# Where the row pieces of a decoder layer stand between its score blocks: one wait moved, activations put at blocks' ends

## The chip, the cores and the metric

The kernel runs on one core of a Trainium2 chip, as one launch. Its engines are TensorE (PE, with its weight loads PEld), VectorE (DVE), ScalarE (ACT), GpSimd (POOL) and SyncE (SP, which here only issues transfers). The metric is the device time of one execution in microseconds; less is better.

## The reference

A post-norm decoder layer in fp32, x of 2 x 1024 x 512, a context of 2 x 2048 x 512: linear attention, cross attention with softmax over 16 heads of 32, and a mixture of 8 experts, each token going to two of them, with a capacity of 640 rows for each expert. Each part is added to its input and normalised.

```python
q = jax.nn.elu(q) + 1.0;  k = jax.nn.elu(k) + 1.0          # linear attention
kv = jnp.einsum('bthd,bthe->bhde', k, v)
out = num / jnp.clip(denom, 1e-06, None)[..., None]
...
dots = jnp.einsum('bhnd,bhmd->bhnm', q, k) * SCALE          # cross attention
attn = jax.nn.softmax(dots, axis=-1)
...
logits = xf @ router_w + router_b                           # experts
topk_p, topk_i = jax.lax.top_k(probs, K)
keep = rank < cap
h = jax.nn.gelu(jnp.einsum('ecd,edf->ecf', buf, w1) + b1[:, None, :], approximate=False)
eo = jnp.einsum('ecf,efd->ecd', h, w2) + b2[:, None, :]
...
x = _layernorm(x + _L0_attn_ref(...)); x = _layernorm(x + _L0_xattn_ref(...)); x = _layernorm(x + _L0_ffn_ref(...))
```

## The kernel before

One Python loop writes a plan, a list of stages with keys, and each engine then walks the whole plan and does its own share of every stage. So the order of the plan is the order in each engine's queue, and semaphores between the engines say when a share may start. The stages of the span, roughly: linear attention and the projections of the context until 540 us, the cross attention loop until 1535, the expert phase until the end.

The loop has 16 turns, each a group of 4 heads by 512 queries, over 2048 keys. A turn has 8 blocks, and each block handles two key tiles (`s`, `s + 1`). The order in a block is the string `BLOCK` (line 50): eight "score" units for the next block, each a matmul of 128 keys by 512 queries that ScalarE turns into exponentials (`score`, line 1834), and eight "max" units, each a matmul whose row maximum VectorE takes (`take_max`, line 1488), for a turn further on. Scores rotate through three PSUM banks, maxima and all side pieces through three others. Behind the units come the numerator matmuls of the current tiles (line 1225), the denominators of an earlier pair (line 1243), now and then ScalarE's copy of a finished numerator or denominator (lines 1841 and 1847), GpSimd's addition of a pair of tiles (line 1956), and VectorE's reciprocals (line 1508). For the last tiles VectorE does the pair additions. The last maxima are over in turn 14, so that the blocks behind it hold scores alone.

The shift of a turn (the row maxima, brought into the query stack) is made of `shift_high`, `shift_low` and `shift`; `shift` is a small TensorE matmul (line 1203) in the maxima's banks, a few blocks after a turn's last maximum.

Between these, "side pieces" finish the rows of (b, h), 512 rows of batch b. A generator, `rows_of`, yields the kind of its next piece, and the block loop takes at most one piece without TensorE in the middle of a block (in front of its tenth unit) and, if none was taken there, one with TensorE at its end; in the last three turns both. The pieces are: the projections of four tiles (`rows`), the router's sums (`parts`), VectorE's inverse roots (`row_root`, `row_shift`), ScalarE's normalisation of each of four tiles (`x2`, line 1853), the logits, the two best experts (`route_top`, in which VectorE subtracts the best logit and ScalarE takes the exponential, line 1866), the counts, ranks, weights and slots, the one-hot matrices (`hot`) and their product (`table`). Three of the four row groups run beside the loop: (0,0) from turn 8, (0,1) from turn 10, (1,0) from turn 13; (1,1) comes behind it.

At the loop's start `second_stack` loads the second stack of keys and what the rows need (`load_xwo`: two weight matrices of 1 MB, three small tables, bxo_cols the last of them). Then `zero_counts` clears three tiles on VectorE and scales the router's weights by bxo_cols, for which it waits for all of `load_xwo`:

```python
dve.wait_ge(*xwo_in[()])
dve.wait_ge(*const_in[()])
V.tensor_tensor(router_scaled[:, :, :], router_pad[:, :, 1:1 + E],
                bxo_cols[:, :].unsqueeze(2).to_broadcast([P, NC, E]), ALU.mult) \
    .then_inc(counts_zero.sem, 1)
```

router_scaled is read by the stage `fold_turn`, in turn 1 (turns count from 0; the change's title calls it turn two).

Of the kernel before, what the change touches and what calls it, by code (L numbers as in the profile page):

```python
# [27 lines left out]
HT = NT // NH  # L28
# [21 lines left out]
BLOCK = 6 * ("max", "score") + ("score", "max", "score", "max")  # L50
WITH_PE, WITHOUT_PE = "with TensorE", "without TensorE"
EARLY, LATE, WHOLE = "early", "late", "whole"
# [71 lines left out]
def program(nc, t):  # L124
    ctx = ExitStack()
    with ctx:
# [165 lines left out]
        def chunk_of(b, mc):  # L292
# [44 lines left out]
        den_summed, den_copied = signal("den_summed"), signal("den_copied")  # L337
        counts_zero, folded = signals_on("fold_done", 2)
        folds_summed, folds_turned = signals_on("folds_summed", 2)
# [56 lines left out]
            "zero_counts": lambda: (counts_zero,),  # L396
            "fold": lambda: (folds_summed, fold_copied),
            "fold_turn": lambda: (folds_turned, folded),
# [20 lines left out]
            "logits": lambda b, h: (logits_summed, logits_done),  # L419
            "route_top": lambda b, h: (logits_shifted, router_exp),  # L420
            "route_counts": lambda b, h: (chosen_ready, before_ready),
# [263 lines left out]
        def rows_of(b, h):  # L685
            yield WITHOUT_PE
            do("fetch_parts", b, h)
            yield from project_rows(b, h, WHOLE)
            yield WITH_PE
            begin_parts(b, h)  # L690
            do("parts", b, h)
            yield WITHOUT_PE
            do("row_root", b, h)
            yield WITHOUT_PE
            do("row_shift", b, h)
            for k in range(HT):
                do("x2", b, h, k)
                if k < HT - 1:
                    yield WITHOUT_PE
            do("store_x2", b, h)  # L700
            yield WITH_PE
            do("logits", b, h, ring=next_s_bank)
            for stage in ("route_top", "route_counts"):
                yield WITHOUT_PE
                do(stage, b, h)
            yield WITH_PE
            do("ranks", b, h, ring=next_s_bank)
            yield WITHOUT_PE
            do("route_weights", b, h)
            yield WITHOUT_PE  # L710
            do("route_slots", b, h)
            for k in range(TOPK):
                yield WITHOUT_PE
                do("hot", b, h, k)
            yield WITH_PE
            do("table", b, h, ring=next_s_bank)
# [22 lines left out]
        clock = 0  # L739
# [98 lines left out]
        shifts = []  # L838

        def due_shifts(until):  # L840
            while shifts and shifts[0][0] <= until:
                shift(shifts.pop(0)[1], next_s_bank)
# [8 lines left out]
        for turn, (n, h) in enumerate(turns):  # L851
            b, g = groups[n]
            stay = stay_of[turn]
            for s in range(0, MT, 2):
# [10 lines left out]
                for u, unit in enumerate(BLOCK):  # L865
                    if u == len(BLOCK) // 2 + 1:
                        busy = side(WITHOUT_PE)
                    if unit == "max":
                        maxima(1)
                    else:  # L870
                        scores((BLOCK[:u].count("score"),))
# [20 lines left out]
                denominators(clock)  # L892
                postponed(clock)
                if not end:
                    do("add_pair", turn, s + 1)
                    pending.append((clock + 1, turn, s + 1))
# [30 lines left out]
        do("logits", b, h, ring=next_s_bank)  # L927
        do("route_top", b, h)
        do("route_counts", b, h)
        do("route_weights", b, h)  # L930
# [118 lines left out]
        def _(_eng):  # L1049
# [100 lines left out]
            def fold_turn():  # L1150
                out = free_bank("fold_turn")
                pe.wait_ge(*fold_copied[()])
                pe.wait_ge(*counts_zero[()])
                for g in range(NG):
# [187 lines left out]
        def _(_eng):  # L1342
# [167 lines left out]
            def zero_counts():  # L1510
                V.memset(before[:, :, :], 0.0)
                V.memset(head_w[:, :, :], 0.0)
                V.memset(table[:, :, :], 0.0)
                dve.wait_ge(*xwo_in[()])
                dve.wait_ge(*const_in[()])
                V.tensor_tensor(router_scaled[:, :, :], router_pad[:, :, 1:1 + E],
                                bxo_cols[:, :].unsqueeze(2).to_broadcast([P, NC, E]), ALU.mult) \
                    .then_inc(counts_zero.sem, 1)

# [187 lines left out]
            def final_dve_rows(q):  # L1707
                dve.wait_ge(*final_root[q // (PIECES_Y // 2)])
                for n in range(q * TILES_Y, (q + 1) * TILES_Y):
# [9 lines left out]
                    "add_pair": add_pair, "invert": invert, "zero_counts": zero_counts, "rows": rows,  # L1719
                    "row_root": row_root, "row_shift": row_shift, "fold_turn": fold_turn, "logits": logits,  # L1720
                    "route_top": route_top, "route_counts": route_counts, "route_weights": route_weights,
# [8 lines left out]
        def _(_eng):  # L1730
# [132 lines left out]

            def route_top(b, h):
                act.wait_ge(*logits_shifted[b, h])
# [35 lines left out]
            def final_act_rows(q):  # L1901
                act.wait_ge(*final_root[q // (PIECES_Y // 2)])
                for n in range(q * TILES_Y, (q + 1) * TILES_Y):
# [9 lines left out]
                    "shift_high": shift_high, "shift": shift, "score": score, "copy_num": copy_num, "copy_den": copy_den, "x2": x2,  # L1913
                    "x1_logits": x1_logits, "fold": fold, "parts": parts, "route_top": route_top, "turn_xe": turn_xe,
                    "split_w1": split_w1,
# [357 lines left out]
```

## Time and profile before

| | |
|---|---|
| median of 3 runs | 2078.73 us (2077.09 to 2081.12) |
| profiled execution | 2077.5 us, its span 2075.7 us |
| TensorE busy | 1934.5 us (93%) |
| VectorE, ScalarE, GpSimd busy | 1224.6, 883.8, 791.5 us |
| chain that ended last | TensorE 79%, VectorE 12%, transfers 3%, ScalarE 2% |
| granted TensorE clock, mean | 0.969 of full |

All rows are from one execution with the profiler, in microseconds from the start of its span. A busy engine is not one at its peak: matmuls overlap, so the start of one to the start of the next says more than their durations. In a row's brackets stands how long its engine (or the queue in front of it) had idled, and who released it.

### The profile page before, as it was taken

How to read it: one execution, taken by the hardware profiler on the slowest of the kernel's cores; microseconds unless marked ns; L12 is line 12 of the kernel's file. 1: busy time of each engine (PE TensorE's matmuls, PEld its weight loads, DVE VectorE, ACT ScalarE, POOL GpSimd, SP SyncE). 2: the span in 40 equal slices, each digit the busy share in tenths (PEclk: the TensorE clock that was granted, in tenths of full speed). 3: DMA queues.
4: the chain of work that ended last, by engine and by line, in shares of the span. 5: the costliest groups of instructions: out<-in, count | busy, mean ns of one | idle time of the engine just before them, and what ended most of it. 6: DMA issues, size and time to landing. Idle time of an engine off the chain costs nothing.

```text
span 2075.7 us, 26455 instructions
## 1 busy us (share of the span) xinstructions
PE 1934.5 (93%) x10152; PEld 1273.9 (61%) x10152; DVE 1224.6 (59%) x2279; ACT 883.8 (43%) x1587; POOL 791.5 (38%) x705
## 2 busy tenths in 40 slices
PE   6999999989499999999999999999988999999992
PEld 5876666677355555555544544544437988889992
DVE  5565553257276787777767867867753444444433
ACT  3212322222165565666546545545734333334431
POOL 3002200000066777777656746756202222322112
PEclk9999999999799999999999999999988999999996
DMA  7002524583602122322324424332224444444415
GB/s 251 30 1 106 178 81 143 184 215 115 185 17 62 37 72 63 80 55 52 94 65 107 97 63 119 91 87 72 82 82 142 132 107 128 132 111 108 117 21 182
DMA packets 119070, 211.04 MB, mean 102 GB/s; under 512 B 10608, under 2 KB 28672, under 8 KB 118864
## 3 DMA queue, kind: packets, MB, share of 16 engines
q1 hardware_dynamic: 108416, 185.39, 30.1%
q0 software_dynamic: 9440, 21.86, 5.4%
q10 hardware_dynamic: 1088, 2.10, 0.3%
q8 instruction: 80, 1.31, 0.3%
q14 instruction: 46, 0.38, 0.1%
HBM read 147.15 MB, written 62.42 MB: 101 GB/s over the span
## 4 chain that ended last, share of the span: by engine, by line
PE 79%; DVE 12%; DMA 3%; ACT 2%; SPq 2%; issue 1%; POOL 0%; ACTq 0%; POOLq 0%; DVEq 0%
PE banks L1059 34%; PE banks L1314 11%; PE banks L1225 11%; PE banks L1195 9%; DVE max L1488 9%; PE banks L1214 7%; PE banks L1243 5%; PE banks L1065 2%; ACT probs_sum L1834 1%; DMA k_parts<-out_lo 1%; DMA wv_raw<-in_wv_t 1%; DMA bxo_cols<-in_bxo_cols 1%; DMA k_half<-in_xwk_t 0%; PE banks L1133 0%; ACT probs_add L1834 0%
## 5 line engine op out<-in xcount | busy, mean ns | idle before, releaser
L1488 DVE TENSOR_REDUCE max<-banks 128x1 f32<-128x512 f32 x1024 | 628.5, 682 | 188.0 <-PE banks L1195 187.4
L1956 POOL TENSOR_TENSOR probs_sum<-probs_sum,probs_add 128x512 f32<-128x512 f32 x464 | 581.9, 1285 | 352.2 <-PE banks L1225 352.2
L1195 PE MATMUL banks<-k_stack,q_stack 98*128 98x512 f32 x1024 | 430.2, 427 | 32.2 <-DVE max L1488 30.6
L1834 ACT ACTIVATE probs_sum<-banks 128x512 f32<-128x512 f32 x512 | 264.9, 604 | 330.4 <-PE banks L1214 329.7
L1214 PE MATMUL banks<-q_stack,k_stack 98*128 98x512 f32 x1024 | 378.4, 400 | 15.1 <-ACT probs_add L1834 14.7
L1195 PEld LDWEIGHTS banks<-k_stack,q_stack 98*128 98x128 f32 x1024 | 192.9, 188 | 222.6 <-DVE max L1488 100.5
L1834 ACT ACTIVATE probs_add<-banks 128x512 f32<-128x512 f32 x512 | 271.9, 612 | 0.5 <-PE banks L1214 0.5
L1214 PEld LDWEIGHTS banks<-q_stack,k_stack 98*128 98x128 f32 x1024 | 192.9, 189 | 75.3 <-ACT probs_add L1834 25.9
L1998 POOL DMA_INDIRECT y_rows<-eo,tok x40 | 79.5, 1987 | 218.1 <-DVE eo L1687 167.6
L1225 PE MATMUL banks<-probs_sum,v_grp 128*32 128x512 f32 x1024 | 142.7, 619 | 0.0
L1225 PE MATMUL banks<-probs_add,v_grp 128*32 128x512 f32 x1024 | 139.1, 605 | 0.0
L1243 PE MATMUL banks<-probs_sum,ones 128*32 128x512 f32 x1024 | 137.2, 598 | 0.8 <-DVE probs_sum L1503 0.8
L1674 DVE TENSOR_TENSOR hid_lo<-hid,hid_hi 128x640 fp32r<-128x640 f32 x64 | 52.8, 826 | 142.4 <-ACT hid_hi L1899 142.4
L1059 PE MATMUL banks<-w_hi,hid_hi 128*128 128x512 f32 x320 | 128.7, 402 | 0.0
L1059 PE MATMUL banks<-w_hi,hid_lo 128*128 128x512 f32 x320 | 126.4, 395 | 0.0
L1059 PE MATMUL banks<-w_lo,hid_hi 128*128 128x512 f32 x320 | 125.9, 393 | 0.0
L1962 POOL TENSOR_TENSOR x_nat<-x_nat,bxo_row 128x512 f32<-128x512 f32 x16 | 21.1, 1350 | 269.6 <-PE banks L1065 269.6
L1314 PE MATMUL banks<-xe_hi,w_hi 128*128 128x320 f32 x512 | 117.7, 311 | 1.5 <-DVE xe_lo L1658 1.5
L1314 PE MATMUL banks<-xe_hi,w_lo 128*128 128x320 f32 x512 | 117.4, 310 | 0.0
L1314 PE MATMUL banks<-xe_lo,w_hi 128*128 128x320 f32 x512 | 117.4, 311 | 0.0
L1894 ACT ACTIVATE hid<-banks,b1c 128x640 f32<-128x640 f32 x64 | 50.8, 794 | 137.1 <-PE banks L1314 137.0
L1989 POOL DMA_INDIRECT xg<-x_rows,tok x40 | 39.2, 979 | 167.0 <-PE banks L1065 134.4
(233 smaller groups left out, 2782.5 us busy)
## 6 DMA issues: line engine op xcount, KB each, us to landing
k_stack<-k_parts SPq DMA_DIRECT2D x144, 256.0 KB, 4.8
w_raw<-in_L_ffn_w SPq DMA_DIRECT2D x16, 2048.0 KB, 8.4
q_stack<-q_parts SPq DMA_DIRECT2D x48, 256.0 KB
v_grp<-v_rows SPq DMA_DIRECT2D x48, 256.0 KB, 3.2
raw<-in_ctx_t SPq DMA_DIRECT2D x8, 1024.0 KB, 6.4
k_parts<-out_hi SPq DMA_DIRECT2D x32, 256.0 KB, 2.5
k_parts<-out_lo SPq DMA_DIRECT2D x32, 256.0 KB, 2.9
v_rows<-pre SPq DMA_DIRECT2D x32, 256.0 KB, 2.3
```

Of the source, the lines that this page charges most:

```text
L1059: done = nc.tensor.matmul(out, lhsT, rhs, start=start and n == 0, stop=stop and n == len(operands) - 1)
L1195: nc.tensor.matmul(out, queries_of(t)[:, j, tile_of(k)], keys_of(t)[0:STK + SHIFT, j, mc * HALF:(mc + 1) * HALF], start=True, stop=True) \
L1214: nc.tensor.matmul(out, keys_of(t)[0:STK + SHIFT, j, tile_of(s)], queries_of(t)[:, j, :], start=True, stop=True).then_inc(scored.sem, 1)
L1225: done = nc.tensor.matmul(bank(NUM)[j * DH:(j + 1) * DH, :], v_grp[:, s, j * DH:(j + 1) * DH], probs_of(t, s)[:, j, :], start=s == 0, stop ...
L1243: done = nc.tensor.matmul(bank(DEN)[j * DH:(j + 1) * DH, :], ones[:, 0:DH], tile[:, j, :], start=s == 1, stop=s == MT - 1 and tile is tile ...
L1314: done = nc.tensor.matmul(pairs[first][:, h, 0:HC], w, x[:, h * HC:(h + 1) * HC], start=n == 0, stop=n == len(terms) - 1)
L1488: V.reduce_max(max4[:, tiles_of(t), :, :][:, k, j, mc:mc + 1], bank(bank_of["max", t, mc, k, j]), AX.X) \
L1674: V.tensor_tensor(hid_lo[:, f, :], hid[f % 2][:, :], hid_hi[:, f, :].bitcast(F32), ALU.subtract) \
L1834: S.activation(probs_of(t, s)[:, j, :], bank(bank_of["score", t, s, j]), ACT.Exp, scale=SCALE) \
L1894: S.activation(hid[f % 2][:, :].rearrange("p (h n) -> p h n", h=2), pairs[first][:, :, 0:HC], ACT.Gelu, bias=b1c[:, e, f:f + 1]).then_inc( ...
L1956: done = G.tensor_tensor(a[:, j, :], a[:, j, :], b[:, j, :], ALU.add)
L1998: G.indirect_dma_start(out=y_rows, in_=eo[turn % EO][:, :], in_offset=None, compute_op=ALU.add, out_offset=bass.IndirectOffsetOnAxis(ap=to ...
```

## The change

Four edits. The scaling of the router's weights leaves `zero_counts` and becomes VectorE's share of the stage `fold`, in turn 1, with a signal of its own, `router_ready`. A third kind of piece, `AT_END`, stands behind a block's numerators and denominators: the normalisations go there, two and two, with the logits between the pairs, and so does the exponential of the logits, as a stage `route_exp` of its own. `row_shift`, `route_top` and `route_counts` stay in mid-block, with VectorE's share alone. And no piece is taken in mid-block where a shift is due at that block's end.

```diff
@@ rows_of
             do("row_shift", b, h)
-            for k in range(HT):
+            yield AT_END
+            for k in range(HT // 2):
                 do("x2", b, h, k)
-                if k < HT - 1:
-                    yield WITHOUT_PE
-            do("store_x2", b, h)
             yield WITH_PE
             do("logits", b, h, ring=next_s_bank)
-            for stage in ("route_top", "route_counts"):
-                yield WITHOUT_PE
-                do(stage, b, h)
+            yield AT_END
+            for k in range(HT // 2, HT):
+                do("x2", b, h, k)
+            do("store_x2", b, h)
+            yield WITHOUT_PE
+            do("route_top", b, h)
+            yield AT_END
+            do("route_exp", b, h)
+            yield WITHOUT_PE
+            do("route_counts", b, h)
             yield WITH_PE
             do("ranks", b, h, ring=next_s_bank)
@@ the block loop
+        def shifts_due(until):
+            return bool(shifts) and shifts[0][0] <= until
...
                     if u == len(BLOCK) // 2 + 1:
-                        busy = side(WITHOUT_PE)
+                        busy = not shifts_due(clock) and side(WITHOUT_PE)
...
                 denominators(clock)
                 postponed(clock)
+                side(AT_END)
                 if not end:
                     do("add_pair", turn, s + 1)
@@ TensorE, fold_turn
                 pe.wait_ge(*fold_copied[()])
-                pe.wait_ge(*counts_zero[()])
+                pe.wait_ge(*router_ready[()])
@@ VectorE
-                V.memset(table[:, :, :], 0.0)
+                V.memset(table[:, :, :], 0.0).then_inc(counts_zero.sem, 1)
+
+            def fold():
                 dve.wait_ge(*xwo_in[()])
                 dve.wait_ge(*const_in[()])
                 V.tensor_tensor(router_scaled[:, :, :], router_pad[:, :, 1:1 + E],
                                 bxo_cols[:, :].unsqueeze(2).to_broadcast([P, NC, E]), ALU.mult) \
-                    .then_inc(counts_zero.sem, 1)
+                    .then_inc(router_ready.sem, 1)
@@ ScalarE
-            def route_top(b, h):
+            def route_exp(b, h):
                 act.wait_ge(*logits_shifted[b, h])
```

VectorE at the loop's start; before, the scaling stands ahead of all reductions of turns 0 and 1:

```order
L1511 MEMSET before 128x40
L1512 MEMSET head_w 128x128
L1513 MEMSET table 128x80
L1516 TENSOR_TENSOR router_scaled<-router_pad,bxo_cols 128x32
L1488 TENSOR_REDUCE max<-banks 128x1 x32
L1495 TENSOR_REDUCE top<-max 128x16
```

The same place after the change:

```order
L1522 MEMSET before 128x40
L1523 MEMSET head_w 128x128
L1524 MEMSET table 128x80
L1499 TENSOR_REDUCE max<-banks 128x1 x32
L1506 TENSOR_REDUCE top<-max 128x16
L1499 TENSOR_REDUCE max<-banks 128x1 x48
L1529 TENSOR_TENSOR router_scaled<-router_pad,bxo_cols 128x32
```

The scaling has moved behind 80 reductions, ten blocks.

ScalarE in turns 8 and 9 beside the rows (0,0), before; each probs row is four exponentials, y_nat rows are normalisations, rt_ex the logits' exponential:

```order
L1834 ACTIVATE probs_sum_53<-banks 128x512 x4
L1853 ACTIVATE y_nat_64<-y_nat_64,neg_shift,rsqrt_y 128x512
L1834 ACTIVATE probs_add_56<-banks 128x512 x4
L1841 ACTIVATE num_c<-banks 128x512
L1834 ACTIVATE probs_sum_54<-banks 128x512 x4
L1853 ACTIVATE y_nat_64<-y_nat_64,neg_shift,rsqrt_y 128x512
L1834 ACTIVATE probs_add_57<-banks 128x512 x4
L1847 ACTIVATE den_c<-banks 128x512
L1834 ACTIVATE probs_sum_55<-banks 128x512 x4
L1853 ACTIVATE y_nat_64<-y_nat_64,neg_shift,rsqrt_y 128x512
```

And after the change:

```order
L1847 ACTIVATE probs_sum_53<-banks 128x512 x4
L1847 ACTIVATE probs_add_56<-banks 128x512 x4
L1854 ACTIVATE num_c<-banks 128x512
L1866 ACTIVATE y_nat_64<-y_nat_64,neg_shift,rsqrt_y 128x512 x2
L1847 ACTIVATE probs_sum_54<-banks 128x512 x4
L1847 ACTIVATE probs_add_57<-banks 128x512 x4
L1860 ACTIVATE den_c<-banks 128x512
L1866 ACTIVATE y_nat_64<-y_nat_64,neg_shift,rsqrt_y 128x512 x2
L1847 ACTIVATE probs_sum_55<-banks 128x512 x4
L1847 ACTIVATE probs_add_58<-banks 128x512 x4
L1879 ACTIVATE rt_ex<-rt_sv 128x32
```

The four normalisations stood in the middle of four blocks' exponentials, and now stand in twos behind two blocks' exponentials and the copy. In (0,1) the two pairs fall behind blocks without a copy, in (1,0) as here. The pieces from the logits to the table come two or three blocks earlier than before. In SyncE's queue the x1 rows for (1,1) come ahead of the first expert's weights, where they stood behind them; the stores of x2 come ahead of a load of values in (0,0), (0,1) and (1,0).

## Rows read from the trace of the kernel before

**Rows 1.** The page: granted TensorE clock in tenths, 40 slices of the span.
```profile
PEclk9999999999799999999999999999988999999996
```
**Rows 2.** Who waited for whom: in total, times, longest.
```profile
DVE router_scaled L1516 <- DMA bxo_cols<-in_bxo_cols: 28.0, 1, 28.0
...
PE banks L1195 <- DVE max L1488: 30.6, 2, 27.8
```
**Rows 3.** Timeline at the loop's start: start, duration, engine, line, what; idle before.
```profile
540.37 0.39 PE L1195 MATMUL banks<-k_stack,q_stack 98*128 98x512 f32 x1
...
542.85 5.88 SPq L2118 DMA_DIRECT2D k_stack<-k_parts  x12
...
557.64 1.19 SPq L2157 DMA_DIRECT2D bxo_cols<-in_bxo_cols  x1
...
569.76 0.80 PE L1195 MATMUL banks<-k_stack,q_stack 98*128 98x512 f32 x1 [27.76 <-DVE max L1488]
...
573.95 1.07 PE L1225 MATMUL banks<-probs_sum,v_grp 128*32 128x512 f32 x8
```
**Rows 4.** Stretches: length, busy of PE, PEld, DVE, ACT, POOL; clock, DMA share, GB/s.
```profile
541.00:569.00 28.00, 1.00 (x5) 0.48 (x3) 0.09 (x1) 1.91 (x4) 0.00 (x0) 0.59 0.92 222
...
679.00:1010.00 331.00, 330.39 (x1940) 170.21 (x1940) 258.55 (x442) 205.85 (x412) 253.70 (x224) 1.00 0.26 61
```
**Rows 5.** The same view: eight plain blocks, parts, three row groups, three single blocks.
```profile
708.91:763.79 54.88, 54.78 (x323) 28.19 (x322) 42.80 (x74) 34.02 (x69) 42.00 (x37) 1.00 0.20 49
965.61:969.71 4.10, 4.10 (x21) 2.77 (x17) 3.57 (x6) 3.93 (x8) 3.55 (x3) 1.00 0.45 96
1475.08:1479.90 4.82, 4.82 (x33) 2.10 (x32) 4.19 (x8) 4.02 (x10) 0.78 (x1) 1.00 0.20 53
1076.13:1179.06 102.93, 96.04 (x551) 48.61 (x550) 82.77 (x183) 60.03 (x118) 68.31 (x60) 0.98 0.43 106
1244.38:1348.63 104.25, 97.30 (x554) 49.30 (x553) 82.83 (x185) 58.66 (x117) 68.46 (x61) 0.97 0.42 105
1413.82:1491.63 77.81, 71.42 (x424) 34.09 (x423) 58.73 (x124) 48.08 (x97) 33.04 (x31) 0.96 0.28 90
1109.97:1117.95 7.98, 7.88 (x50) 4.42 (x49) 6.37 (x12) 4.80 (x10) 5.43 (x5) 1.00 1.03 307
1302.46:1310.07 7.61, 7.51 (x45) 3.93 (x44) 7.47 (x17) 4.84 (x10) 5.44 (x5) 1.00 0.13 34
1339.70:1348.63 8.93, 8.83 (x58) 5.31 (x57) 8.06 (x16) 4.78 (x10) 5.44 (x5) 1.00 0.83 178
```
**Rows 6.** Timeline, TensorE's waits in turns 8 and 9 beside the rows (0,0).
```profile
1085.39 0.77 PE L1214 MATMUL banks<-q_stack,k_stack 98*128 98x512 f32 x1 [2.87 <-ACT probs_add L1834]
...
1125.23 0.50 PE L1214 MATMUL banks<-q_stack,k_stack 98*128 98x512 f32 x1 [0.89 <-ACT probs_add L1834]
...
1134.46 0.30 PE L1203 MATMUL banks<-identity,max_parts 128*32 128x128 f32 x1 [1.69 <-DVE max L1488]
```
**Rows 7.** ScalarE: first exponentials behind num_c, behind den_c, behind neither; the normalisations' group.
```profile
959.56 0.60 ACT L1834 ACTIVATE probs_sum<-banks 128x512 f32<-128x512 f32 x1 [0.90 <-PE banks L1214]
...
966.38 2.06 ACT L1834 ACTIVATE probs_sum<-banks 128x512 f32<-128x512 f32 x4
...
973.18 2.06 ACT L1834 ACTIVATE probs_sum<-banks 128x512 f32<-128x512 f32 x4 [2.75 <-PE banks L1214]
...
L1853 ACT ACTIVATE y_nat<-y_nat,neg_shift,rsqrt_y 128x512 f32<-128x512 f32 x12 | 10.0, 830 | 7.0 <-DVE neg_shift L1555 7.0
```
**Rows 8.** VectorE, one instruction of route_counts: (0,0), and (1,0) without maxima beside.
```profile
1132.69 0.19 DVE L1589 TENSOR_TENSOR rt_ms<-rt_chosen 128x32 f32<-128x32 f32 x1
...
1459.28 1.18 DVE L1589 TENSOR_TENSOR rt_ms<-rt_chosen 128x32 f32<-128x32 f32 x1
```
**Rows 9.** Issue of the first expert's weights, and ScalarE's first split of them.
```profile
1482.26 0.43 SPq L2189 DMA_DIRECT2D w_raw<-in_L_ffn_w  x1
...
1498.70 1.13 ACT L1880 ACTIVATE w_hi<-w_raw 128x1024 fp32r<-128x1024 f32 x1
```

More of the change, by code:

```diff
@@ L50 @@
 BLOCK = 6 * ("max", "score") + ("score", "max", "score", "max")
-WITH_PE, WITHOUT_PE = "with TensorE", "without TensorE"
+WITH_PE, WITHOUT_PE, AT_END = "with TensorE", "without TensorE", "at the end of a block"
 EARLY, LATE, WHOLE = "early", "late", "whole"
@@ L337, in program @@
         den_summed, den_copied = signal("den_summed"), signal("den_copied")
-        counts_zero, folded = signals_on("fold_done", 2)
+        counts_zero, router_ready, folded = signals_on("fold_done", 3)
         folds_summed, folds_turned = signals_on("folds_summed", 2)
@@ L396, in program @@
             "zero_counts": lambda: (counts_zero,),
-            "fold": lambda: (folds_summed, fold_copied),
+            "fold": lambda: (folds_summed, fold_copied, router_ready),
             "fold_turn": lambda: (folds_turned, folded),
@@ L419, in program @@
             "logits": lambda b, h: (logits_summed, logits_done),
-            "route_top": lambda b, h: (logits_shifted, router_exp),
+            "route_top": lambda b, h: (logits_shifted,),
+            "route_exp": lambda b, h: (router_exp,),
             "route_counts": lambda b, h: (chosen_ready, before_ready),
@@ L838, in program @@
         shifts = []
+        def shifts_due(until):
+            return bool(shifts) and shifts[0][0] <= until
         def due_shifts(until):
-            while shifts and shifts[0][0] <= until:
+            while shifts_due(until):
                 shift(shifts.pop(0)[1], next_s_bank)
@@ L928, in program @@
         do("route_top", b, h)
+        do("route_exp", b, h)
         do("route_counts", b, h)
@@ L1719, in _ @@
                     "add_pair": add_pair, "invert": invert, "zero_counts": zero_counts, "rows": rows,
-                    "row_root": row_root, "row_shift": row_shift, "fold_turn": fold_turn, "logits": logits,
+                    "row_root": row_root, "row_shift": row_shift, "fold": fold, "fold_turn": fold_turn, "logits": logits,
                     "route_top": route_top, "route_counts": route_counts, "route_weights": route_weights,
@@ L1913, in _ @@
                     "shift_high": shift_high, "shift": shift, "score": score, "copy_num": copy_num, "copy_den": copy_den, "x2": x2,
-                    "x1_logits": x1_logits, "fold": fold, "parts": parts, "route_top": route_top, "turn_xe": turn_xe,
+                    "x1_logits": x1_logits, "fold": fold, "parts": parts, "route_exp": route_exp, "turn_xe": turn_xe,
                     "split_w1": split_w1,
```

## The prediction

> **What bounds the kernel.** I read the page's slices first. The TensorE clock row shows 9 nearly everywhere and one 7 in the middle [rows 1]: TensorE sets the pace, with one break. The list of waits names the break: VectorE waited 28.0 us, once, for the transfer of bxo_cols, and TensorE waited 27.8 us in one piece for VectorE's maxima [rows 2]. The timeline shows the order: the first score block begins at 540.37; SyncE issues the second key stack from 542.85 and bxo_cols, the last of that burst, at 557.64; TensorE goes on at 569.76, and the block's numerators start at 573.95 [rows 3]. In 541 to 569 the DMA engines were 92% busy with 222 GB/s; over the 331 us from 679 to 1010 TensorE was busy 330.39 us at full clock [rows 4].
>
> Then I cut the loop at the starts of the numerator matmuls (line 1225), one start per block. Eight plain blocks of a turn take 54.88 us, 6.86 each; the scores-and-maxima part of one is 4.10; a block without maxima takes 4.82 [rows 5]. The three stretches in which a group of rows goes from row_shift to table take longer than their blocks alone: that difference is what the rest of the change can touch.
>
> **Part 1, router_scaled moved to turn two.** It removes one wait and moves one small VectorE instruction (0.19 us for one of its size [rows 8], beside TensorE's work). Without the wait the first block is one like any other: begun at 540.37, its numerators would start 4.10 later, at 544.5. They started at 573.95, so 29.5 us go: 27.8 of wait, the rest matmuls at the low clock after it. The clock was granted at 0.59 over 541 to 569 [rows 4], that is mostly 1.2 GHz, after TensorE had stopped; the first matmul after it took 0.80 us in its row against 0.39 for the same form at 540.37 [rows 3].
> The Trainium skill ("TensorE: Matmul & The Clock Gate", Part 1) says that the low clock is the state of an idle array and that activity lifts it. The trace agrees; by that rule the gain is the wait and a restart, by the wait alone it would be 27.8.
>
> What is late next? The loop reads only stack 0, queries 0 and 1 and values that landed long before. The second stack is first read by turn two's maxima: 32 of turn one's 64 maxima are left, 4 blocks, so about 540.4 + 4 x 6.86 = 568. The stack (16 transfers of 256 KB with its queries, some 4 MB) stands ahead of the 2 MB of weights; at 222 GB/s it is in by about 541 + 18 = 559. Hidden, with 9 us to spare. If transfers slowed to half their rate beside the running engines it would be in at 577, and the cost 9 us: that is the other end. router_scaled itself now waits for the weights at the second block of turn one, about 607; they landed by 569. No queue is moved past: SyncE issues the same burst in the same order.
>
> **Part 2, the side pieces.** Before: (rows 0,0) 102.93 us for 13 blocks, 13 x 6.86 = 89.2, excess 13.7. (0,1) 104.25, excess 15.1. (1,0) 77.81 for 5 blocks with maxima and 6 without: 34.3 + 28.9 = 63.2, excess 14.6 [rows 5]. Sum 43.4.
> Of it TensorE's own matmuls stay: the logits block 7.98 - 6.86 = 1.1, the ranks block 7.61 - 6.86 = 0.75, the table block 8.93 - 6.86 = 2.1 [rows 5]; 3.95 for each of three, 11.8. That leaves 31.6 that come from where the pieces stand. Three kinds show in the waits [rows 6]: TensorE 2.87 us for ScalarE, whose normalisation stood mid-block waiting for row_shift with the exponentials queued behind it (and low clock after it); 0.89 for ScalarE with the logit exponential mid-block; 1.69 of a shift matmul for VectorE's maxima behind route_counts. The change takes each of these places away: the two activations go behind the block's exponentials, VectorE's pieces lose their ScalarE half, and none starts beside a due shift.
>
> What comes in. Two normalisations now stand in a row behind a block's exponentials: 2 x 0.83 = 1.66 us [rows 7]. In a plain block ScalarE idles 2.75 us there, so they are free; behind the numerator copy it idles 0.90, so they cost 0.76; behind the denominator copy no idle time is shown before the exponentials (the row at 966.38 has no bracket), so they cost the full 1.66 [rows 7]. I carry this over to TensorE in full, since its third score bank is taken just as it comes free. Groups (0,0) and (1,0) meet both copies, (0,1) none: 2 x 2.42 = 4.8. Bounds: 0, if the banks absorb it, and 8 x 0.83 = 6.6, if nothing does.
> VectorE's row_shift (7 small instructions, as row_root has) stays mid-block alone; I take 0 for it, between 0 and 2.9 for three (the waits above were ScalarE's). In (1,0) route_counts and ranks share a block, and TensorE must wait for the counts: 1.1, and 1.0 for a slow clock behind it; between 0 and 4. The remaining neighbours (two reciprocals beside route_counts, ranks beside a shift) 1.0, between 0 and 3. Sum of new costs 7.9. Gain 31.6 - 7.9 = 23.7.
>
> At route_counts a rule speaks. The row rt_ms took 0.19 us at 1132.69 and 1.18 at 1459.28 [rows 8], the second in a block without maxima. It has two inputs in SBUF. GpSimd's four pair additions fill 42.00 of the 54.88 us of a plain turn [rows 5], 5.25 of each 6.86, from a little behind the numerators' start; the middle of a block with maxima lies just behind them, that of a block without maxima within them. In the new order of (1,0) this piece moves from the second kind to the first.
> The Trainium skill ("SBUF — State Buffer", SBUF: two separate sides) says VectorE instructions with two SBUF inputs and GpSimd's lock each other out for a whole instruction. By that rule a piece in mid-block of a full block, when GpSimd's four additions are over, is cheap; the row pair agrees. By it the wait for the counts in (1,0) could be near nothing, 2 us less than my sum; I keep the sum.
>
> SyncE's queue is changed too: x1 rows for (1,1) now stand ahead of the first expert weights, 1 MB. Both, 3 MB, were issued at 1482.3, and at the 222 GB/s of the first burst they are in by 1496; ScalarE's first split of the weights ran at 1498.70 [rows 9]. The new schedule is 2 us shorter between the two (the table block is gone from there), so 0.7 us of cover is left: I take nothing, at worst the 1 MB, 4.7 us.
>
> **Sum.** 29.5 + 23.7 = 53.2. The profiled execution took 2077.5 (span 2075.7), so 2024.3 for its like; the median of before is 2078.73, 1.2 above it. I forecast 2025.
>
> **Rivals.**
> (a) The side pieces' gain is mostly lost: normalisations in pairs hold the exponentials, the block stretches, VectorE's pieces fall into GpSimd's additions. For it: the copies' row without idle time. Against: only four of six pairs meet a copy. With new costs at their upper ends (6.6 + 2.9 + 4 + 3 = 16.5) the gain is 15.1 and the time 2034; with half of the old excess kept as well, 2040.
> (b) The burst takes VectorE's place as the bound: TensorE waits for the second stack at about 568. For it: 92% busy DMA engines. Against: the stack is first in the queue. Price 9: 2034.
> (c) More than forecast: the pairs are absorbed, and counts away from GpSimd's additions gives up to 4. New costs near 1: 2017.
> (d) Slower. The place is the stretch after 541: the 28 us of rest is gone and TensorE runs through at full load, and the granted clock sinks for the rest. TensorE is busy nearly all the time in the 1535 us behind it. The gain of 53 is used up where the clock of these is down by 53/1535 = 3.5%; at 4.5% the time is 2094. Against: 331 us without a pause were granted 1.00 [rows 4].
> (e) The change does not do what it says: router_scaled waits again in turn one. It would need weights landing after 607 instead of by 569. Then about 2055 with part 2 alone.
>
> **Chances.** Forecast (2019 to 2031) 0.60; (a) 0.14; (b) 0.06; (c) 0.14; (d) 0.03; (e) 0.03. For its range I take the forecast, (b), most of (c) and the near half of (a): 2016 to 2036. 0.2% is 4.2 us, about what this kernel's runs can tell from no change. Faster 0.96, same 0.01, slower 0.03.
>
> **What would show it.** In the profile of the changed kernel: no wait of VectorE for bxo_cols over 1 us, no 7 in the clock row at 540, numerators of the first block at about 544.5, and the first plain turn's blocks still 6.86. The end of the early rows (the block at 1491.63 before) near 1438. From the numerators ahead of row_shift's block to those behind table's block (0,0) has 11 blocks now, 11 x 6.86 + 3.95 + 2.4 = 81.8 us; (0,1) has 10 and no copies, about 73. TensorE's longest wait for ScalarE's exponentials under 2 us, one in the block with the denominator copy of turns 9 and 14. The tail from the last numerators to the end unchanged within 2 us. I am wrong on part 1 if TensorE waits for k_stack or q_stack near 568, and wrong on part 2 if blocks 9 and 14 with the pairs stretch by more than 2 us each.

## The result, and the profile after

The changed kernel takes 2019.82 us (median of 4 runs, 2017.9 to 2024.36) against 2077.91 for the kernel before, run beside it (4 runs, 2074.19 to 2081.12): ratio 0.9724, 95% interval 0.9701 to 0.9747. The forecast was 2025, its range 2016 to 2036. The profiled execution of after took 2017.9 (span 2016.1); before it was 2077.5 (span 2075.7), so 59.6 us went.

The clock row of after answers to [rows 1]: the 7 behind the first quarter is gone. The 7 late in the row comes from behind the loop, as the 88 did before: there TensorE is busy 9 of 22 us and is granted half of its clock in both kernels.
```profile
PEclk9999999999999999999999999999979999999996
```
Stretches behind the loop, columns as in [rows 4], before (first line) and after:
```profile
1548.00:1570.00 22.00, 9.03 (x36) 7.36 (x36) 13.25 (x54) 5.59 (x9) 6.66 (x7) 0.50 0.46 158
```
```profile
1490.00:1512.00 22.00, 8.60 (x35) 7.15 (x36) 13.13 (x56) 5.87 (x10) 6.38 (x7) 0.50 0.47 156
```
The waits of TensorE from 540 to 1480, the whole loop, answer to [rows 2]: neither the 27.8 us nor any wait for bxo_cols is left.
```profile
PE banks L1070 <- DVE max L1499: 1.7, 1, 1.7
PE banks L1225 <- ACT probs_sum L1847: 1.6, 2, 0.8
PE banks L1254 <- DVE probs_sum L1514: 0.8, 1, 0.8
```
The timeline at the loop's start, against [rows 3] (lines stand 11 to 13 further down in after). The first block begins at 538.81 instead of 540.37 and its numerators follow 4.24 us later, not 33.58. The multiply now stands at 605.11 and waits for nothing.
```profile
538.81 0.39 PE L1206 MATMUL banks<-k_stack,q_stack 98*128 98x512 f32 x1
...
543.05 0.64 PE L1236 MATMUL banks<-probs_sum,v_grp 128*32 128x512 f32 x4
...
605.11 0.18 DVE L1529 TENSOR_TENSOR router_scaled<-router_pad,bxo_cols 128x32 f32<-128x32 f32 x1
```
Stretches of after, columns as in [rows 4]. The first is the stretch of the burst: TensorE busy 28.00 of 28.00 at full clock, beside transfers at 218 GB/s. Then the stretches from row_shift's block to the table block of rows (0,0), 11 blocks, and (0,1), 10 blocks; then four single blocks: row_shift (0,0); second pair of normalisations behind the denominator copy; counts and ranks of (1,0); the one behind it.
```profile
541.00:569.00 28.00, 28.00 (x159) 14.41 (x158) 21.08 (x37) 18.09 (x37) 20.22 (x17) 1.00 0.91 218
1043.56:1124.44 80.88, 79.80 (x472) 41.58 (x471) 71.06 (x162) 50.99 (x101) 57.42 (x50) 1.00 0.49 122
1189.62:1262.38 72.76, 72.46 (x431) 38.36 (x430) 66.07 (x155) 46.91 (x92) 52.45 (x46) 1.00 0.45 116
...
1043.56:1050.38 6.82, 6.82 (x41) 3.45 (x40) 6.54 (x16) 4.06 (x9) 5.45 (x5) 1.00 0.79 172
...
1058.35:1066.35 8.00, 7.22 (x42) 3.30 (x41) 5.46 (x25) 5.15 (x10) 5.00 (x4) 1.00 0.69 201
...
1385.03:1394.16 9.13, 7.43 (x45) 3.96 (x44) 8.21 (x19) 4.92 (x11) 5.44 (x5) 1.00 0.53 170
1394.16:1402.67 8.51, 8.51 (x42) 3.80 (x41) 5.14 (x13) 3.33 (x7) 5.42 (x5) 0.80 0.00 0
```
Predicted for the two long stretches were 81.8 and about 73; they are 80.88 and 72.76. Row_shift's block, 10.39 before, is a plain one. The block that stood at 1491.63 and was foretold near 1438 is at 1433.91.

I name a block by the turn and the first key tile of the numerators that end it: row_shift (0,0) is (8,14), the denominator copy with a pair (9,2) and (14,2), counts with ranks (14,4). Cut at these starts, the profiled executions of all kernels repeat themselves where the work is the same: from (1,6) to (8,12) all fourteen took 422.01 to 422.13 us. Outside the loop they don't. In the eleven that don't wait for bxo_cols, the first numerators start between 540.11 and 545.65; from block (15,2) to the end of the span all fourteen take 582.2 to 585.4. Between them, blocks (1,4) and (1,6) and those beside the rows vary from execution to execution by 1 to 3 us. So a difference of a few us in whole times is no reading of the change, and the experiments below are read by their blocks. Their ratios are to the kernel before, run beside them: its median was 2074.88 for experiments 1, 2 and 7, 2074.07 for 4, 5 and the first of 6, and 2076.12 for 3, the second of 6, and 8.

Where the 59.6 us of the two profiled executions came from:
```
                                         before     after     gone
start of the loop's first numerators     573.95    543.05    30.90
blocks (1,4) and (1,6), the fold          18.17     16.56     1.61
other blocks up to (8,12)                484.01    483.95     0.06
(8,12) to (15,2), the row groups         415.50    390.35    25.15
(15,2) to the end of the span            584.07    582.19     1.88
```

### The profile page after: what moved, and what is told of

The parts are those of the page before. It is cut to its first block, busy times and chain, and to the rows that moved or that the text cites. A ratio compares the mean times of both kernels' runs of the same rounds, so it can differ in the third digit from the quotient of the medians.

```text
span 2016.1 us, 26457 instructions
## 1 busy us (share of the span) xinstructions
PE 1919.1 (95%) x10152; PEld 1268.9 (63%) x10152; DVE 1221.2 (61%) x2279; ACT 882.5 (44%) x1587; POOL 793.8 (39%) x705
## 4 chain that ended last, share of the span: by engine, by line
PE 85%; DVE 10%; DMA 2%; ACT 1%; issue 1%; SPq 0%; POOL 0%; ACTq 0%; POOLq 0%; DVEq 0%
PE banks L1070 36%; PE banks L1236 11%; PE banks L1325 11%; PE banks L1206 10%; PE banks L1225 9%; DVE max L1499 7%; PE banks L1254 5%; PE banks L1076 2%; DMA k_parts<-out_lo 1%; DMA wv_raw<-in_wv_t 1%; DVE stats_y L1707 0%; PE banks L1144 0%; DVE src_lo L1369 0%; DVE wq_lo L1375 0%; ACT src_hi L1754 0%
## 5 line engine op out<-in xcount | busy, mean ns | idle before, releaser
L1697 DVE TENSOR_TENSOR eo<-banks,b2s 128x512 f32<-128x512 f32 x40 | 27.7, 692 | 126.6 <-PE banks L1070 126.6
```

## Experiments

**1. The parts alone.** Part 1 on the kernel before:
```
  V.memset(table[:, :, :], 0.0).then_inc(counts_zero.sem, 1)
+ def fold():
+     dve.wait_ge(*xwo_in[()])   # and the multiply, on router_ready
```


> The kernel before with the first part of the change alone (router_scaled computed at the first fold piece of turn one, with a signal of its own). Theory: the wait of 27.8 us and the restart at the low clock go (30.9 us at the first block's numerators in the changed kernel), and with them the low clock in the fold blocks of turn one (10.09 and 8.08 us before, 9.74 and 6.82 in the changed kernel), so 32.6 us in all: about 2045. Rival: the 1.7 us of the fold blocks come from the second part or from chance; then these blocks measure 10.1 and 8.1 again and the time is about 2047. Second rival: the parts work together (less is gained alone); then over 2050.

Measured: 2046.46 (4 runs), ratio 0.9859 (0.9839 to 0.9880); numerators from 543.23; (1,4) and (1,6) 9.74 and 8.46, where the theory had 9.74 and 6.82 and the rival 10.1 and 8.1, so neither held for both; from (8,12) to (15,2) 417.24, as before but for one slow block. The first part is worth its wait and no more: 30.7 us at the start, of which 29.3 lie in the first block (538.99 to 543.23).

And the changed kernel with part 1 undone, the same edit backwards:

> The changed kernel with the first part undone: router_scaled stands in the loop's first block again, the second part stays. Theory: VectorE waits 28 us for bxo_cols and TensorE 27.8 us for a maximum as before, the fold blocks of turn one measure 10.1 and 8.1 us, and the side blocks keep all of their 25.1 us: about 2052, or 2050 if the 1.9 us behind the loop come too. Rival: the side blocks gain less when the schedule is 32 us later against the DMA transfers; then 2055 or more.

Measured: 2050.71 (4 runs), ratio 0.9887 (0.9866 to 0.9909). The wait is back, TensorE's only one over 2 us in the loop:
```profile
PE banks L1206 <- DVE max L1499: 28.0, 1, 28.0
```
The fold blocks took 9.73 and 8.52, not the 10.1 and 8.1 of the kernel before. The row groups took 388.67 us, 26.8 less than before. By blocks the parts don't work on each other: 30.7 and 26.8 make 57.5, the changed kernel has 30.90 + 25.15 = 56.05, and the block (14,6), 8.51 there and 6.81 here, is as long as the difference (more of it below). Whole times can't show it to a few us: the two medians stand 28.4 and 24.2 us below the kernel before, 52.6 in sum.

**2. Place in the queue, or the multiply itself?** The kernel before, the multiply where it was:
```
  do("load_bxo")        # first of the burst, on a semaphore of its own;
                        # the multiply waits for that one alone
  do("one_rows", 1)
```


> The kernel before, with bxo_cols issued first in the burst on a semaphore of its own; the multiply stays in the loop's first block and waits for this transfer alone. Theory (the cost was the place in the queue, 14.8 us behind the burst's start and behind its bytes): the transfer lands some 3 us after its issue at about 542.5, VectorE waits under 5 us and TensorE under 2 us; 28 to 32 us go, 2046 to 2050. Rival 1: the burst itself or the multiply at this place holds the block up; then at least half of the 30 us stays, 2063 or more. Rival 2: a short wait is enough to drop the clock, and 5 to 10 us stay: 2051 to 2057.

Measured: 2046.89 (4 runs), ratio 0.9862 (0.9842 to 0.9883). VectorE's wait, and TensorE's two in 535 to 560:
```profile
DVE router_scaled L1518 <- DMA bxo_cols<-in_bxo_cols: 0.7, 1, 0.7
```
```profile
PE banks L1197 <- DVE max L1490: 0.5, 1, 0.5
PE banks L1216 <- ACT probs_sum L1836: 0.5, 1, 0.5
```
The transfer was issued at 541.67 and had landed at 543.26; before, it was issued at 557.64 and had landed at 568.89. The cost was what the transfer stood behind, not the burst beside the loop nor the multiply at its place. This run moved two things at once, the place in the queue and the semaphore, which the kernel before shares with the 2 MB of weights; issued first but on the shared semaphore, the multiply would still wait for the weights, which landed at 567.22. Done so, issuing the small transfer first is worth as much as moving the multiply (2046.89 against 2046.46 in experiment 1).

**3. How much cover has the second key stack?** The changed kernel with the 2 MB of weights ahead of it:
```
- do("one_rows", 1); load_q(2); load_k(1, 0..3); do("load_xwo")
+ do("load_xwo"); do("one_rows", 1); load_q(2); load_k(1, 0..3)
```


> The changed kernel with the 2 MB of weights (xwo, lane_no, col_no, bxo_cols) issued ahead of the second key stack, so that the stack lands some 9 us later (2 MB at 218 GB/s): a test of how much cover the stack has, now that TensorE no longer stands still. Theory: the maxima read the stack in its four parts, the first at about 569 and each next one two blocks later; with 9 us to spare for the first and more for the others nothing waits, 2019 to 2021, and the blocks up to (0,8) measure 6.8 as in the changed kernel. Rival: the cover is just the 9 us that the prediction worked out or less, and TensorE waits 1 to 5 us near 568: 2021 to 2025.

Measured: 2018.7 (4 runs), ratio 0.9721 (0.9707 to 0.9736), no wait and no longer block up to (8,12). The stretch of the burst:
```profile
541.00:569.00 28.00, 28.00 (x167) 14.07 (x170) 21.07 (x36) 17.72 (x36) 20.28 (x17) 1.00 0.84 193
```
Counted from the loop's first numerators, the stack landed 6 to 7 us later than in the changed kernel, and not the 9 expected: its first quarter 14.2 us behind them instead of 7.0, its last 24.8 instead of 18.6. The maxima read it quarter by quarter, the first from some 22 us behind these numerators (an estimate from the block starts) and each next one two blocks later. So 8 us of cover were left for the first quarter, more for the others, and the prediction, which wanted the whole stack by the first read, had counted too little cover. Rival (b) had less ground than the 6% I gave it.

**4. The activations' places.** First the logit exponential mid-block again:
```
  do("route_top", b, h)
- yield AT_END
  do("route_exp", b, h)
```


> The changed kernel with the logit exponential back in the middle of the block, with route_top. Theory: ScalarE waits in the middle of the block for VectorE's shifted logits with the probabilities' exponentials queued behind, as before (7.94 to 7.96 us for a block with route_top against 6.82): 1.1 us in each of three blocks, 3.4 us more than the changed kernel, about 2023. Rival: the cost of route_top's block before was VectorE's part, which the change leaves mid-block at no cost in (11,6): then under 0.5 us in all, 2020.

Measured: 2021.86 (4 runs, 2019.61 to 2027.6), ratio 0.9740 (0.9723 to 0.9756), whose interval overlaps that of the changed kernel. The blocks tell it: (9,2) 8.41 for 8.00, (11,6) 8.17 for 6.82, (14,2) 8.41, (14,4) 9.57 for 9.13, and (14,6) 9.59 for 8.51, 3.7 us in all. In the two blocks where the pair already holds the exponentials up, the second hold costs only 0.4. The theory's 3.4 us were to come from (9,2), (11,6) and (14,2), 1.1 each; these gave 2.2, and the other 1.5 came from (14,4) and (14,6), granted 0.94 and 0.70. That the sums agree is luck.

Then the normalisations mid-block:
```
  do("row_shift", b, h)
- yield AT_END
  for k in range(HT // 2): do("x2", b, h, k)      # the second pair behind route_top likewise
```


> The changed kernel with the normalisations back in mid-block: the first pair directly behind row_shift, the second behind route_top (in (1,0) all that follows stands one block earlier, since nothing waits for a block's end there). Theory: the first pair waits for row_shift with the exponentials queued behind it, 3.6 us in its block and 1.7 in the next, as before; the second pair has nothing to wait for and costs twice the 0.62 us that a single one cost in mid-block before (7.44 against 6.82). Per group 5.3 + 1.2, three groups 19.5, less the 2.3 us of the pair behind the denominator copy: 17 us more, about 2037. Rival: most of it was ScalarE's busy time rather than the wait; then both pairs cost the same, 1.2 to 1.7 us each: 7 us more, 2027.

Measured: 2039.2 (4 runs), ratio 0.9827 (0.9808 to 0.9846). The blocks of row_shift: 10.92, 10.82, and 12.61 with the logits; those behind them 1.3 and 2.3 longer; the pair with nothing to wait for (11,6) 8.13, 1.3 over a plain block. 18.3 us in the row groups where 17 were expected: the wait is the larger part.
```profile
1054.92 0.61 PE L1223 MATMUL banks<-q_stack,k_stack 98*128 98x512 f32 x1 [3.57 <-ACT probs_add L1845]
```

**5. The shifts.** `busy = side(WITHOUT_PE)`, without the rule:

> The changed kernel without the rule that no VectorE piece starts beside a due shift: route_slots (0,0), route_weights (0,1) and row_root (1,0) then stand in the blocks of the shifts of turns 10, 12 and 14, and what follows them stands one block earlier. Theory: VectorE is late with the maxima behind the piece and the shift's matmul waits for it, as beside the counts (8.59 us) and the hot columns (8.85 us) before, against 7.0 for a block with a shift alone: 1.6 us in each of three blocks, 4.8 us more, about 2024.6. Rival: only the counts and the hot columns are long enough for it, the other pieces are free: under 1 us in all, 2020 to 2021. By 2% of the time neither is told apart; the blocks' own lengths are.

Measured: 2025.55 (4 runs), ratio 0.9760 (0.9742 to 0.9778), 7.8 us more in the row groups. The blocks with slots, weights and row_root beside a shift: 8.82, 8.45, 8.68; and two of the next at a clock of 0.80, 8.70 and 8.69.
```profile
PE banks L1214 <- DVE max L1499: 5.3, 3, 1.9
```
The three blocks are 1.8, 1.5 and 1.7 over one with a shift alone (7.0), 5.0 in all where the theory had 4.8; the low clock behind two of them adds 3.4, and the pieces moved by one block give some 0.6 back. So the rule is worth something for short pieces too, and the rival fell.

**6. Which normalisation pair costs?** The second pair behind the logit exponential, one block on:
```
  yield AT_END
  do("route_exp", b, h)
+ for k in range(HT // 2, HT): do("x2", b, h, k)
```


> The changed kernel with the second pair of normalisations moved one block on, behind the logit exponential, so that no pair stands behind the denominator copy. Theory: the 1.2 us by which the blocks (9,2) and (14,2) exceed a plain one came from the pair, which held the exponentials behind the copy; both go to 6.8, and the exponential with the pair (0.3 + 1.5 us of ScalarE) is hidden in the next block, as ScalarE idles 2.75 us there: 2.3 us less than the changed kernel, 2017.5. Rival: route_top on VectorE beside the denominator copy costs it: the blocks stay at 8.0. Second rival: three activations in a row are too many, and the next blocks ((9,4), (11,8), (14,4)) grow by 0.5 to 1 us each: no gain.

Measured: 2017.96 (4 runs), ratio 0.9724 (0.9708 to 0.9740). (9,2) and (14,2) fell from 8.0 to 6.89 each, so the pair behind den_c cost 1.11, not route_top. (9,4) and (14,4) did not grow, (11,8) did, from 6.81 to 7.85. ScalarE's timeline there:
```profile
1215.74 0.23 ACT L1824 ACTIVATE max_parts<-top 128x16 fp32r<-128x16 f32 x1 [2.23 <-DVE top L1505]
1215.88 0.21 ACT L1878 ACTIVATE rt_ex<-rt_sv 128x32 f32<-128x32 f32 x1
1216.00 1.51 ACT L1865 ACTIVATE y_nat<-y_nat,neg_shift,rsqrt_y 128x512 f32<-128x512 f32 x2
...
1218.04 0.50 PE L1224 MATMUL banks<-q_stack,k_stack 98*128 98x512 f32 x1 [0.66 <-ACT probs_sum L1846]
```
ScalarE's queue held its copy for shift_high first, which waits for VectorE's top; 2.23 us of its idle time were spent on that wait, and the pair came behind it. Neither theory had this.

All four behind one end:
```
- for k in range(HT // 2): do("x2", b, h, k)
+ for k in range(HT): do("x2", b, h, k)
```


> The changed kernel with all four normalisations (3.0 us of ScalarE) behind one block's end: behind the numerator copy in groups (0,0) and (1,0), behind a plain block in (0,1). Theory: what holds TensorE is only how much later than the first score bank the exponentials start; a pair (1.5 us) was hidden behind both kinds of block, four exceed ScalarE's 2.75 us of idle time by 0.3 in the plain block and its 0.90 by about 2.1 behind the copy, less what the banks give (0.6 as read from the pair there). So (11,4) grows by 0 to 0.5, (9,0) and (14,0) by 1.3 to 1.5 each, and (9,2) and (14,2) fall from 8.0 to 6.9: in all within 1 us of the changed kernel. Rival: the cost is that of the copies' blocks whatever stands behind them; then (9,0) and (14,0) stay at 7.97 and 2.2 us are gained, 2017.7. Second rival: the third bank gives nothing beyond a pair: each block 1.5 us more, 4.5 less 2.2: 2022.

Measured: 2024.77 (4 runs), ratio 0.9758 (0.9742 to 0.9775). The plain block (11,4) took all four at no cost, 8.01 as with two. Behind the numerator copy they cost 2.84 and 2.59 us, twice what I expected:
```profile
1052.29 2.92 ACT L1863 ACTIVATE y_nat<-y_nat,neg_shift,rsqrt_y 128x512 f32<-128x512 f32 x4
1055.11 2.03 ACT L1844 ACTIVATE probs_sum<-banks 128x512 f32<-128x512 f32 x4
1055.75 0.50 PE L1222 MATMUL banks<-q_stack,k_stack 98*128 98x512 f32 x1 [1.34 <-ACT probs_sum L1844]
...
1058.12 0.63 PE L1222 MATMUL banks<-q_stack,k_stack 98*128 98x512 f32 x1
```
The same block as a stretch, columns as in [rows 4]:
```profile
1049.81:1060.62 10.81, 9.47 (x50) 5.70 (x49) 7.95 (x18) 8.12 (x15) 4.98 (x4) 0.85 0.67 217
```
The wait is the 1.3 expected; the rest is the low clock behind it (0.63 for a matmul of 0.40, the block granted 0.85). In the first group the next block still had 0.79 and took 8.61 for 6.88. So the row groups took 4.9 us more than in the changed kernel, where the theory had at most 1: it had the wait right and no clock in it.

**7. Counts and ranks of (1,0) in separate blocks.** The rule that lets a block take both kinds, not in block (14,4):
```
- if not busy or turn >= LAST - 2:
+ if not busy or turn >= LAST - 2 and (turn, s) != (LAST - 1, 4):
```


> The changed kernel, with the ranks of rows (1,0) one block behind its counts (both shared a block of turn 14, 9.13 us, and the next took 8.51 with the clock at 0.67). Theory: the ranks' matmul no longer waits 1.70 us for VectorE and the clock stays at 1.00; the two blocks go to 6.8 and 7.6, the pieces behind them move one block and cost nothing there: 3.2 us less than the changed kernel, about 2016.6. Rival: the clock falls there for another reason (GpSimd's lock or the shift), then 1.5 us less; second rival: the pieces moved by one block (weights into a block without maxima, fetch of the x1 rows one block later, the first expert weights' issue) cost 1 to 3 us again: no gain.

Measured: 2018.57 (5 runs, 2014.71 to 2024.23), ratio 0.9729 (0.9707 to 0.9751): by whole times not told apart from the changed kernel. By blocks 6.82 and 7.91 for 9.13 and 8.51, 2.9 us, and the pieces moved behind cost nothing.

**8. A better order, and the changed kernel again.** The edits of 7 and of 6 together, 6 for (0,0) and (1,0) only:
```
+ if h:                       # (0,1): second pair ahead of route_top
+     yield AT_END; second_pair()
  ...
+ if not h: second_pair()     # behind route_exp
```


> A candidate for a better kernel: the changed one with the ranks of (1,0) a block behind its counts, and the second pair of normalisations of (0,0) and (1,0) behind the logit exponential instead of the denominator copy ((0,1) stays, since there the next block's queue holds shift_high, for which ScalarE waited 2.23 us with the pair behind it). Theory: 1.1 us less in each of (9,2) and (14,2), and 1.2 to 2.9 in (14,4) with (14,6), according to whether the clock falls there; 3.4 to 5.1 less than the changed kernel in the same call, of which runs can tell little. Rival: a third activation behind the exponential in (14,4) is too much in one of the blocks: 1 us less gained.

> The changed kernel unaltered, for comparison on the same chip. Theory: the blocks that came out 1.7 us longer in some runs ((1,6) behind the small fold matmuls, 6.82 in its first profile and 8.5 in four of the others; (14,6) behind the 1.7 us wait, 8.51 in its first profile and 6.81 in two others with the same wait) differ from execution to execution: at least one of the two differs from its first profile, while all others agree within 0.1 us. Rival: they belong to the kernel: 6.82 and 8.51 again.

Measured: combined 2016.46 (5 runs, 2015.83 to 2018.44), ratio 0.9714 (0.9701 to 0.9727); the changed kernel again 2020.84 (5 runs, 2017.44 to 2021.67), ratio 0.9728 (0.9715 to 0.9742). The medians stand 4.4 apart, the intervals of the ratios overlap; the row groups took 385.14 against 390.26 us, 5.1 less. I take the combined one for the better by its blocks; by whole times it isn't certain.

The repeat had (1,6) at 8.93 instead of 6.82, (1,4) at 10.90 instead of 9.74 (as in the second of experiment 4, 10.88), and (14,6) at 8.47, as in the changed kernel's first profile. Over all fourteen profiled executions (1,6) took 6.81 or 6.82 in four (the changed kernel's first, and experiments 3, 5 and the first of 6) and 8.08 to 8.96 in ten. (14,6) took 8.5 to 9.6 in five of the kernels in which counts and ranks share the block ahead of it, and 6.81 in two (the second of experiment 1 and the first of 6) behind the same wait of 1.7 us. My expectation that nothing else would differ failed for (1,4).

## Why the prediction was right, step by step

**Part 1: right.** 29.5 forecast; the first block's stretch went from 33.58 (540.37 to 573.95) to 4.24 (538.81 to 543.05), 29.3. The other 1.56 of the 30.90 lie ahead of the loop and are within what this varies. The stack was covered, though it landed at 561.7 and not by 559, and VectorE's multiply waited for nothing.

**Part 2: right in place, 1.5 us low in size**, 25.15 against 23.7. The size itself varies between executions: the row groups took 414.7 to 417.2 us in the three profiles with the old order, 388.7 to 390.4 in the four with the new one (the changed kernel twice, the second of experiment 1, experiment 3), so 24.3 to 28.6 went.
- Row_shift mid-block alone: 0 forecast, 0 measured.
- The pairs of normalisations: 0.76 behind the numerator copy and 1.66 behind the denominator copy forecast, 0 and 1.11 measured, in two groups each: 4.8 forecast, 2.2 measured. The step that failed is "carry this over to TensorE in full": of the forecast's terms the banks take all of the 0.76 and some 0.5 of the 1.66. A smaller part is the pair itself, 1.51 us and not 2 x 0.83. Row against row, from the changed kernel: behind num_c the pair left the first exponentials at 1054.28 and TensorE did not wait; behind den_c they began at 1063.11 and it waited 0.78.
```profile
1052.87 1.51 ACT L1866 ACTIVATE y_nat<-y_nat,neg_shift,rsqrt_y 128x512 f32<-128x512 f32 x2
...
1054.28 2.04 ACT L1847 ACTIVATE probs_sum<-banks 128x512 f32<-128x512 f32 x4
...
1061.20 0.60 ACT L1860 ACTIVATE den_c<-banks 128x512 f32<-128x512 f32 x1 [2.94 <-PE banks L1254]
...
1061.70 1.51 ACT L1866 ACTIVATE y_nat<-y_nat,neg_shift,rsqrt_y 128x512 f32<-128x512 f32 x2
...
1063.11 2.04 ACT L1847 ACTIVATE probs_sum<-banks 128x512 f32<-128x512 f32 x4
...
1063.74 0.50 PE L1225 MATMUL banks<-q_stack,k_stack 98*128 98x512 f32 x1 [0.78 <-ACT probs_sum L1847]
```
- Counts and ranks of (1,0) together: 1.1 and 1.0 forecast; 9.13 is 1.56 over a plain block with ranks (6.82 + 0.75), and the next block 1.69 over. The wait, and the slow matmuls behind it (1.89 for 1.04):
```profile
1391.82 0.19 DVE L1602 TENSOR_TENSOR rt_ms<-rt_chosen 128x32 f32<-128x32 f32 x1
...
1392.86 1.89 DVE L1499 TENSOR_REDUCE max<-banks 128x1 f32<-128x512 f32 x3
...
1393.60 0.41 PE L1070 MATMUL banks<-rt_ms,earlier 128*128 128x32 f32 x2 [1.70 <-DVE max L1499]
1393.85 0.39 PE L1070 MATMUL banks<-before,ones 128*128 128x32 f32 x2
1394.16 1.89 PE L1236 MATMUL banks<-probs_sum,v_grp 128*32 128x512 f32 x8
```
The piece rt_ms took 0.19 here and 1.18 before [rows 8]. The Trainium skill ("SBUF — State Buffer", SBUF: two separate sides) has VectorE's instructions with two SBUF inputs and GpSimd's exclude each other; the trace agrees with the shorter piece: GpSimd had ended at 1391.71 here, and before it was adding from 1457.89 to 1462.88, all around the longer one. But my conclusion from it, that the wait could be near nothing, fell. VectorE began the counts at 1391.27, ended them at 1392.82, 0.9 us after TensorE had run out of work, and then took the next maximum, and the ranks' matmul also needs a bank that a maximum frees: that made the 0.9 into 1.70. The forecast's 1.1 had the counts alone.
- The other neighbours: 1.0 forecast. Ranks beside shift_high and two reciprocals took 7.92 instead of 7.60, and table (0,1) 9.26 instead of 8.93: 0.65. The new costs found so are 2.2, 3.25 and 0.65, 6.1 against 7.9 in the sum.
- SyncE's order: 0 forecast; the weights were issued at 1427.02, the first split ran at 1440.99, and the blocks around it are as long as before.

**What was not in the sum.** 6.4 us more went than forecast: 1.4 from part 2, and 5.0 from three places that the change doesn't touch (1.56 ahead of the loop, 1.61 in the fold blocks, 1.88 behind the loop). The repeat and the other kernels show that these vary between executions: the 582.19 behind the loop is the shortest of all fourteen. The prediction's own mechanisms give 29.3 + 25.2 = 54.5, near 2023 from this profile's 2077.5; that the first profile went 5 us below is luck, and the repeat of experiment 8 stands 55.3 below the kernel before (2076.12 to 2020.84).

**Rivals.** (a) and (b) fell by the block table and experiment 3; (c) was right in one of its two grounds, and in part: the pairs were absorbed by 2.6 of 4.8 us, the counts gave nothing, and the new costs were 6.1, not near 1; (d) fell, the granted clock over the span rose from 0.969 to 0.982; (e) fell with the timeline. In (a), with half of the old excess of 31.6 kept as well, the time would be 2034 + 15.8 = 2050, not 2040.

## What to carry to other kernels

A tiny operand behind megabytes in a queue, or on a semaphore shared with them, costs the whole burst if an engine waits for it that feeds the bound one; here moving the reader and moving the transfer were worth the same. Side work on an engine that feeds the bound belongs where nothing of it has to wait: behind its own urgent work, and only as long as its idle time there, counted after everything else that its queue holds at that place. Small gains are read from stretches that repeat, since the whole time varies by several us for other reasons.

## What the runs showed of the hardware that was not expected

- A short wait can cost double. In the loops of the fourteen profiles TensorE waited 1.3 to 2.0 us twenty times. Behind twelve of these the granted clock (1.00 is 2.4 GHz, 0.50 is 1.2) was 0.70 to 0.85 over a block, at a cost of 1.3 us and more each (beside a wait of 1.3, in experiment 6); behind eight it stayed 1.00. Two of three waits of 1.2 us were followed by a low clock, none of those of 1.13 us and less; and one of 2.6 us, in experiment 2, was not either. The same wait of 1.7 us was followed by 8.51 us in the changed kernel and by 6.81 in two others.
- The clock also fell where the profile has TensorE busy almost throughout. In the repeat of the changed kernel the block of the fold's 8-column matmuls and the next:
```profile
603.96:614.86 10.90, 10.79 (x68) 7.34 (x60) 6.10 (x12) 4.66 (x9) 5.44 (x5) 0.88 0.35 87
614.86:623.79 8.93, 8.93 (x42) 3.76 (x41) 4.76 (x11) 3.33 (x7) 5.42 (x5) 0.76 0.05 11
```
The Trainium skill ("TensorE: Matmul & The Clock Gate", Part 1) ties the low clock to an idle array; here the profile shows none idle, only small matmuls. What decides between 6.82 and 8.93 in equal code was not found, and spreading these matmuls was not tried.
